# Cross-attention: the product of probabilities and values every second step, both value tiles in one PSUM bank, keys in two banks, the output read by one operation of ScalarE and one of VectorE

## What is computed

```python
q, k, v = proj(hs, Wq, bq, S), proj(at, Wk, bk, T), proj(at, Wv, bv, T)
scores = jnp.clip(jnp.einsum('bhsd,bhtd->bhst', q, k) / 4.0, -50.0, 50.0)
scores = jnp.clip(jnp.where(attend, scores, -10000.0), -50.0, 50.0)
probs = jax.nn.softmax(scores, axis=-1)
probs = probs / (probs.sum(axis=-1, keepdims=True) + 1e-08)
ctx = jnp.einsum('bhst,bhtd->bhsd', probs, v).transpose(0, 2, 1, 3).reshape(B, S, H)
delta = layernorm(rs * (ctx @ Wo.T + bo)) * ln_gamma + ln_beta
```

## Time and profile before

| what | us |
|---|---|
| median of three runs | 1716.51 |
| lowest and highest of the three | 1715.1 and 1719.35 |
| the profiled execution's own time | 1717.53 |
| its span (first to last instruction) | 1715.2 |

### The profile page before, as it was taken

The page is one execution under the profiler, slowest core; times in us unless marked ns, Lnnn a source line. Parts: engine busy times, 40 slices in busy tenths (PEclk is TensorE's granted clock), DMA queues, the critical chain, the costliest instruction groups (busy, mean ns, idle before and its releaser), DMA issues. The chain is left out here.

```text
span 1715.2 us, 45769 instructions
## 1 busy us (share of the span) xinstructions
PE 1561.6 (91%) x18290; PEld 1320.9 (77%) x18290; DVE 1402.8 (82%) x2513; ACT 1122.1 (65%) x2171; POOL 746.5 (44%) x727
## 2 busy tenths in 40 slices
PE   5899999998746999999999999999999999999455
PEld 5888888887535888888888888888888888888234
DVE  3788777787375889889899899898898898898687
ACT  3565555565344777777777777777777777777474
POOL 1566555565144344434434434444344354343014
PEclk9999999999677999999999999999999999999777
DMA  6000000000041111111111111111111111110001
GB/s 192 2 1 2 2 2 0 1 1 0 1 147 46 49 41 50 50 50 49 50 46 43 49 50 50 49 50 50 43 51 44 50 49 50 50 50 2 1 11 33
DMA packets 41613, 66.69 MB, mean 39 GB/s; under 512 B 7749, under 2 KB 40194, under 8 KB 41282
## 3 DMA queue, kind: packets, MB, share of 16 engines
q1 hardware_dynamic: 41410, 63.93, 12.9%
HBM read 62.08 MB, written 1.84 MB: 37 GB/s over the span
## 5 line engine op out<-in xcount | busy, mean ns | idle before, releaser
L1144 POOL TENSOR_TENSOR xa_CW<-xa_CTX,xa_CH 128x500 fp32r<-128x500 f32 x187 | 305.4, 1633 | 592.6 <-ACT xa_CH L1338 592.6
L1366 DVE TENSOR_TENSOR xl_ACC<-xl_ACC,xl_PB 125x896 f32<-125x896 f32 x320 | 438.3, 1370 | 11.0
L1330 ACT ACTIVATE xl_PB<-banks,xl_BIB,xl_SCB 125x896 f32<-125x896 f32 x384 | 401.0, 1095 | 32.1 <-PE banks L1202 31.7
L1357 DVE TENSOR_SCALAR xl_PB<-xl_PB 125x896 f32<-125x896 f32 x384 | 249.6, 650 | 64.1 <-ACT xl_PB L1330 63.0
L1312 ACT ACTIVATE xl_V<-banks 125x256 f32<-125x256 f32 x384 | 147.4, 384 | 155.3 <-PE banks L1169 155.3
L1169 PE MATMUL banks<-xa_WVhigh,xa_CH 128*125 128x256 f32 x768 | 238.6, 311 | 0.0
L1169 PE MATMUL banks<-xa_WVlow,xa_CH 128*125 128x256 f32 x768 | 216.0, 281 | 0.0
L1169 PE MATMUL banks<-xa_WVhigh,xa_CW 128*125 128x256 f32 x768 | 215.9, 281 | 0.0
L1303 ACT ACTIVATE xl_KXhigh<-banks,xa_bk 128x500 fp32r<-128x500 f32 x192 | 130.4, 679 | 100.4 <-PE banks L1169 100.4
L1218 PE MATMUL banks<-xl_PB,xl_V 125*32 125x112 f32 x6144 | 187.2, 262 | 1.5 <-DVE xl_PB L1357 1.5
L1373 DVE SCALAR_TENSOR_TENSOR xl_KXlow<-banks,xa_bk,xl_KXhigh 128x500 fp32r<-128x500 f32 x192 | 137.4, 715 | 55.0 <-ACT xl_KXhigh L1303 54.4
(11 more groups left out here) (234 smaller groups left out, 3954.6 us busy)
## 6 DMA issues: line engine op xcount, KB each, us to landing
xa_CTX<-in_ctxT SPq DMA_DIRECT2D x93, 500.0 KB, 3.6
fw_WO<-in_W_o SPq DMA_DIRECT2D x1, 2048.0 KB, 17.7
xq_WR<-in_w_gating SPq DMA_DIRECT2D x1, 2048.0 KB, 9.7
X<-in_x SPq DMA_DIRECT2D x1, 1792.0 KB, 10.2
out<-ff_R SPq DMA_DIRECT2D x16, 112.0 KB, 1.9
fw_QUT<-in_W_quT SPq DMA_DIRECT2D x1, 1536.0 KB, 12.5
xa_CTX<-in_ctxT SPq DMA_DIRECT2D x1, 1500.0 KB, 15.0
xq_WL<-in_w_linear SPq DMA_DIRECT2D x1, 1024.0 KB, 11.8
```

What stands on the lines that cost most here:

```text
L1144: nc.gpsimd.tensor_tensor(context_piece(CW, i), context_piece(CTX, i), context_piece(CH, i), ALU.subtract).then_inc(ctx_low, 1)
L1330: nc.scalar.activation(PB[t % PR][:, :, :], banks[0:TK, 2 * i:2 * i + KT, 0:QW], ACT.Exp, scale=SCB[j][:, t:t + 1], bias=BIB[j][:, t:t + 1 ...
L1357: nc.vector.tensor_scalar(pt, pt, E_HI, E_LO, ALU.min, ALU.max).then_inc(clipped, 1)
L1366: nc.vector.tensor_tensor(ACC[j][:, :, :], prev[:, :, :], PB[t % PR][:, :, :], ALU.add).then_inc(summed, 1)
```

## The change

- The product is done every second step (at odd `u - 1`) for the four tiles of two steps. PB and V have six places for that, and the waits of ScalarE on `pv_done` count pairs of steps.
- Both value tiles of a step go into bank 4 and are read by one copy of 512 columns. A tile's projection waits for the copy of the step before (`v_ready`).
- Keys take banks 5 and 7 in turn, and wait for the low part two keys back instead of one.
- `project` comes at the end of step 3, behind the keys, and `read_delta` in step 4; the keys of step 4 wait for it. NORM and ADD_DELTA shift by one step, but the last of ADD_DELTA stays at s = 9, and the wait for `x_added` at s = 10.
- The output in bank 6 is read by one operation of ScalarE (first heads, 224 columns, behind the exponentials of u = 0) and one of VectorE (second heads, behind add 1 of u = 0). Before, VectorE did four operations of 112 columns between add 0 and clip 1. The product of u = 2 waits for it, where that of u = 1 did.
- `spread_queries` moves from u = 1 to 3 and `mask_columns` from u = 2 to 4.
- One copy of two columns falls away (bn_aggr writes into MV3).

```diff
-PR = 4
+PR = 6
...
-    V_BANK, O_BANK, K_BANK = (4, 5), 6, 7
+    V_BANK, O_BANK, K_BANK = 4, 6, (5, 7)
+    D_BANK = K_BANK[1]
...
-    PROJECT, NORM, ADD_DELTA = 3, {4: (0, 1), 5: (2,), 6: (3,), 10: (4, 5), 11: (6,)}, (6, 8, 9)
+    PROJECT, NORM, ADD_DELTA = 3, {5: (0, 1), 6: (2,), 7: (3,), 10: (4,), 11: (5,)}, (7, 8, 9)
...
-        V = [sb(f"V{i}", [TK, H]) for i in range(PR)]
+        V = sb("V", [TK, PR, H])
...
-        OM = sb("OM", [P, KT, S])
-        DM = sb("DM", [P, KT, S])
-        OR = sb("OR", [P, KT, S])
-        DR = sb("DR", [P, KT, S])
+        OM = sb("OM", [P, 2 * KT, S])
+        ODR = sb("ODR", [P, 2 * KT, S])
+        OR, DR = ODR[:, 0:KT, :], ODR[:, KT:2 * KT, :]
...
+        def output_by_head():
+
+            return bank[O_BANK][:, 0:2 * KT * PAIR_COLS].rearrange("p (k h s) -> p k h s", k=2 * KT, h=2)
...
-                            if u == 1:
+                            if u == 3:
...
-                            if u == 2:
+                            if u == 4:
...
-                    split_products(bank[K_BANK][:, 0:CK], lambda a, kt: WK[a][:, kt, m * P:(m + 1) * P],
+                    split_products(bank[K_BANK[p % 2]][:, 0:CK], lambda a, kt: WK[a][:, kt, m * P:(m + 1) * P],
...
-                def values(n, u, tiles, early=False):
-
-                    for i in tiles:
+                def values(n, u):
+
+                    if n:
+                        pe.wait_ge(v_ready, n)
+                    for i in range(2):
                         t = 2 * u + i
-                        if not early:
-                            pe.wait_ge(v_ready, n * 2 + i - 1)
-                        split_products(bank[V_BANK[i]][0:TK, 0:H], lambda a, kt: ctx_parts[a][:, kt, t * TK:(t + 1) * TK],
-                                       lambda a, kt: WV[a][:, kt, :]).then_inc(v_done, 1)
+                        mm = split_products(bank[V_BANK][0:TK, i * H:(i + 1) * H], lambda a, kt: ctx_parts[a][:, kt, t * TK:(t + 1) * TK],
+                                            lambda a, kt: WV[a][:, kt, :])
+                    mm.then_inc(v_done, 1)
...
                 def values_product(n, u):
 
-                    pe.wait_ge(v_ready, n * 2 + 2)
-                    for i in range(2):
+                    pe.wait_ge(v_ready, n + 1)
+                    for i in range(-2, 2):
                         t = 2 * u + i
                         pe.wait_ge(clipped, n * 2 + i + 1)
                         for kt in range(KT):
                             for c in range(GROUPS):
                                 mm = nc.tensor.matmul(
                                     bank[O_BANK][c * 32:(c + 1) * 32, kt * PAIR_COLS:(kt + 1) * PAIR_COLS],
-                                    V[t % PR][:, kt * P + c * 32:kt * P + (c + 1) * 32],
+                                    V[:, t % PR, kt * P + c * 32:kt * P + (c + 1) * 32],
...
-                        mm = nc.tensor.matmul(bank[K_BANK][0:T, 0:H], CN[:, kt, :], WO[:, kt, :], start=(kt == 0), stop=(kt == KT - 1))
+                        mm = nc.tensor.matmul(bank[D_BANK][0:T, 0:H], CN[:, kt, :], WO[:, kt, :], start=(kt == 0), stop=(kt == KT - 1))
...
-                            if pu == 0 and not (first and j == 0):
-
-                                pe.wait_ge(d_read, b)
-                            values_product(n - 1, pu)
+                            if pu == 1 and not (first and j == 0):
+
+                                pe.wait_ge(o_read, b)
+                            if pu % 2 == 1:
+                                values_product(n - 1, pu)
                             if pu == STEPS - 1:
                                 denominators(b - 1, 1 - j)
                         if more(last, s, 1):
-                            values(n + 1, (u + 1) % STEPS, (0,))
-                        if s == PROJECT and not first:
-
-                            pe.wait_ge(k_ready, n + K_AHEAD)
-                            project(g - 1)
-                        if more(last, s, 1):
-                            values(n + 1, (u + 1) % STEPS, (1,))
+                            values(n + 1, (u + 1) % STEPS)
                         if more(last, s, K_AHEAD):
 
-                            pe.wait_ge(k_ready, n + K_AHEAD)
-                            if s == PROJECT and not first:
+                            pe.wait_ge(k_ready, n + K_AHEAD - 1)
+                            if s == PROJECT + 1 and not first:
                                 pe.wait_ge(delta_ready, g)
                             i = (s + K_AHEAD) % STEPS
                             if i % KT == 0:
                                 pe.wait_ge(ctx_low, n + K_AHEAD + KT - C_AHEAD)
                             keys(n + K_AHEAD, i)
+                        if s == PROJECT and not first:
+
+                            pe.wait_ge(k_ready, n + K_AHEAD)
+                            project(g - 1)
...
+                def first_heads(b):
+
+                    act.wait_ge(pv_done, (b * STEPS + STEPS) // 2)
+                    act.wait_ge(den_done, b + 1)
+                    if b:
+                        act.wait_ge(o_read, b)
+                    nc.scalar.activation(OM[:, :, :], output_by_head()[:, :, 0, :], ACT.Copy, scale=D2[:, 0:1]).then_inc(o_half, 1)
...
-                def values_out(n, u, early=False):
-
-                    if not early:
-                        act.wait_ge(pv_done, n - 1)
-                    for i in range(2):
-                        act.wait_ge(v_done, n * 2 + i + 1)
-                        nc.scalar.activation(V[(2 * u + i) % PR][:, :], bank[V_BANK[i]][0:TK, 0:H], ACT.Copy).then_inc(v_ready, 1)
+                def values_out(n, u):
+
+                    if n >= 3:
+                        act.wait_ge(pv_done, (n - 1) // 2)
+                    act.wait_ge(v_done, n + 1)
+                    t = 2 * u % PR
+                    nc.scalar.activation(V[:, t:t + 2, :], bank[V_BANK][0:TK, 0:2 * H].rearrange("t (i h) -> t i h", i=2), ACT.Copy).then_inc(v_ready, 1)
...
-                            if not (first and s < 2):
-                                act.wait_ge(pv_done, n - 1)
+                            if n >= PR // 2:
+                                act.wait_ge(pv_done, (n - 1) // 2)
...
+                        if u == 0 and not (first and j == 0):
+                            first_heads(b - 1)
...
-                        if s == 5 and not first:
+                        if s == 6 and not first:
...
                 def read_output(b):
 
-                    src = by_head(0)
-                    dve.wait_ge(pv_done, b * STEPS + STEPS)
-                    dve.wait_ge(den_done, b + 1)
-                    nc.vector.tensor_scalar(OM[:, :, :], src[:, :, 0, :], D2[:, 0:1], None, ALU.mult).then_inc(o_half, 1)
                     dve.wait_ge(o_half, b + 1)
-                    nc.vector.scalar_tensor_tensor(out=OR[:, :, :], in0=src[:, :, 1, :], scalar=D2[:, 1:2], in1=OM[:, :, :],
+                    nc.vector.scalar_tensor_tensor(out=ODR[:, :, :], in0=output_by_head()[:, :, 1, :], scalar=D2[:, 1:2], in1=OM[:, :, :],
                                                    op0=ALU.mult, op1=ALU.add).then_inc(o_read, 1)
-                    src = by_head(KT * PAIR_COLS)
-                    nc.vector.tensor_scalar(DM[:, :, :], src[:, :, 0, :], D2[:, 0:1], None, ALU.mult).then_inc(d_half, 1)
-                    dve.wait_ge(d_half, b + 1)
-                    nc.vector.scalar_tensor_tensor(out=DR[:, :, :], in0=src[:, :, 1, :], scalar=D2[:, 1:2], in1=DM[:, :, :],
-                                                   op0=ALU.mult, op1=ALU.add).then_inc(d_read, 1)
...
-                        if before and u == 0:
-                            read_output(b - 1)
...
-                        if s == PROJECT and not first:
+                        if s == PROJECT + 1 and not first:
...
+                        if before and u == 0:
+                            read_output(b - 1)
```

43 lines of the change are left out of this document (19 added, 24 removed).

## The result

The changed kernel takes 1727.35 us (median of 5 runs, 1725.92 to 1729.45), the kernel before 1716.51 beside it: ratio 1.0062, 95% interval 1.0046 to 1.0077. It is slower by about 10.8 us, with 1720 forecast and a range of 1702 to 1738.

A forecast was written before the change was run, and what follows sets the result against it. TensorE, busy 399.5 of 400 us, was taken to bound the loop, with VectorE close at 89%. Terms -12.5 - 1.5 + 1.0 + 16.7 = +3.7 gave 1721.2, forecast as 1720 for the runs' median; range 1702 to 1738.

The forecast's parts named there:

- likeliest case: The forecast itself, whole kernel: gain and new waits of like size, 1712 to 1728 us, chance 0.45.
- Product every second step: TensorE's product blocks: 0.12 to 0.14 us saved for each of 96 that fall away, taken as 12.5 us gained.
- Keys in two banks: Loop start: the second keys' wait of 1.54 us for VectorE's low part goes, 1.5 us gained.
- Project and read_delta: Keys of step 4 wait 0.31 us for VectorE's read, against 0.24 in step 3 before: 1 us lost.
- the bad end of the bound: Keys of step 4: one more add held up by GpSimd before VectorE's read, 15 us lost.
- Values in one bank, output read: ScalarE's copy of the values has 1.9 us of cover, the output read a whole step: no cost.
- GpSimd's order: Later X makes VectorE's last clip and add late; step 0's product and denominators wait 1.11 us a pair, 16.7 lost.
- backlog carried further: Slower rival: VectorE falls behind in odd steps, one more GpSimd meeting per pair; 1735 to 1745 us, chance 0.18.
- The faster rival: VectorE meets GpSimd less between steps 10 and 0 and catches up in time: 1703 us, chance 0.30.

The follow-up runs named there:

- e12: The kernel of e9 with the keys in one bank again (bank 7) and the delta in bank 5: 1723.58 us.
- e2: The changed kernel with VectorE's read_delta first in step 4, ahead of clip 0 instead of behind add 0: 1717.59 us.
- e4: The changed kernel with VectorE's wait for the addition into X, and its statistics of X, at step 11 instead of 10: 1726.00 us.
- e1: The changed kernel with spread_queries back at u = 1 and mask_columns back at u = 2: 1724.43 us.
- e7: The changed kernel with the wait for X at step 11 and read_delta first in step 4: 1715.94 us.
- e10: The kernel of e8 with GpSimd's spreading of queries cut from 448 columns to 16 after the first pair, output not the reference's: 1703.98 us.
- e8: The kernel of e7 with the denominators of a batch behind the values of step 0 instead of ahead of them: 1715.78 us.
- e9: The kernel of e7 with values ahead of the product in steps 0 and 6, and denominators behind that product: 1700.76 us.

## Why the prediction was right, and where it was off

The time, 1727, lies in the range and 7 us above the forecast. It is in the likeliest case, 1712 to 1728, just under its edge; that the kernel would be slower had the chance 0.36, as much as no difference. By its steps:

- **Product every second step**: right. 1.67 for four tiles (1.68), steps of 4.46 and 6.13 (4.47 and 6.17), 0.140 us a block, the upper of the two values that I gave: -13.4 against -12.5.
- **Keys in two banks**: the wait is gone (-1.5), but the start gained 3.9, with a clock that rose earlier. A term of the size 2.4 was missing (e12, with one bank again, lost 3.3 there). The prediction also saw no such wait later in the loop, which is so at steps of 5.39; at steps of 4.5 the second bank is what keeps it so (17.8 us in e12).
- **Project and read_delta**: right place, too small. The wait is 0.62, not 0.31. The add ahead of the read takes 1.70 instead of 1.09, beside the second spreading operation (`QB1low`), and though clip 0 came earlier, the read ends 5.17 after its step and not 4.92. The text had this as the bad end of the bound; e2 showed that moving the read ahead of the add takes all of it back.
- **Values in one bank, output read**: no wait of TensorE on either in the profile after. The copy of 512 columns takes 0.60 (0.68 estimated), the merged read 0.45. ScalarE itself waits at its new read of the output, 33.8 us in all from 550 to 1600 us, which the text had not looked at; it cost nothing that TensorE shows. No experiment took these parts alone.
- **GpSimd's order**: the mechanism held, X at 10.27 after step 9 (9.7), clip 0 of step 10 at 5.83 (5.2), last clip of step 11 at 18.60 (18.16), denominators late by 0.72 (0.73), product by 0.19 (0.38), in 14 pairs and not 15. What failed was the list of who waits: the low keys of step 10, queued behind those clips, are wanted by the scores of step 0. That is 0.65 us a pair, 9.1 us, more than the net miss, in a term that the sum did not have. It also covers part of the product's wait, which comes after it: 0.19 here, 0.75 in e4, where the scores are on time. And the deeper cause, which I named only as a rival ("backlog carried further"), is the one that the runs bear out: putting X back early (e1) or no longer waiting for it (e4, e7) gave 3 us and about 1, because the same time turned up at the next wait; freeing VectorE of its meetings in steps 9 and 10 (e10) gave 11.8, against e8.
- **The faster rival**, 1703: the time is there, 1700.8, but not by chance of phase. It takes the read of the delta, the norm step and the product of the last step at other places (e9).

The forecast was near for one more reason that was no merit: the start and the blocks gained 3.3 more than I put down, the keys of step 4 and the waits of step 0 cost 8.8 more, and so over a third of the miss cancelled.

## What to carry to other kernels

When the steps of a pipeline are made shorter or uneven, list everything that waits behind a late instruction on its engine, the small ones too (here 0.73 us of low keys), and who asks for each. When an engine at 90% is late at one point, an operation that somebody waits for can go ahead of one that nobody waits for yet (e2: the whole wait came back). Moving work or idle time about within the late stretch only moves the wait (e1, e4): there take work or contention away (e10), or let the other engine ask later (e9), and put a price on the new place (here 0.20 to 0.31 us for a block between two others that did well side by side). With the three edits of e9 the gain of the shorter stream came through: 1700.8 from 1727.4.
